# Attention's ramp in a fused attention and tree-FFN kernel: idle products, a split query moved to VectorE, values in another bank, later sums

## What is computed

```python
msg  = h_neigh + E[adj]                       # per target and neighbour
q    = layernorm(x) @ Wq.T + bq               # 8 heads of 16
k, v = msg @ Wk.T + bk, msg @ Wv.T + bv
s    = where(adj == 0, -1e9, q.k / 4)
x    = x + (softmax(s) masked @ v) @ Wo.T + bo
# tree of depth 7: each token takes one path of 8 nodes
h = layernorm(x)
for level in range(8):
    score = h . w1s[node] + b1s[node]
    out  += (h @ w2s[node] + b2s[node]) * gelu(|score|)
    node  = 2 * node + 1 + (score > 0)
x = x + out
```

## Time and profile before

| | us |
|---|---|
| runs of the kernel before | 143.86, 144.15, 145.56; median 144.15 |
| the profiled execution, its whole time | 144.65 |
| its span (first to last record) | 142.70 |
| outside the span | 1.95 |
| busy in the span: PE, DVE, ACT, POOL | 108.8, 98.2, 64.2, 40.4 |
| scores of unit 0 start, end of attention's unit loop on VectorE | 12.23, 62.63 |
| mean granted clock of TensorE | 0.923 of full speed |

### The profile page before, as it was taken

One profiled execution on the slowest core, in us unless ns is written; L12 is line 12 of the kernel. 1 busy time (PEld: TensorE's weight loads), 2 busy tenths in 40 slices (PEclk: granted clock), 3 DMA queues, 4 the chain that ended last, 5 costly groups with the idle time before them and its releaser, 6 DMA issues.

```text
span 142.7 us, 3388 instructions
## 1 busy us (share of the span) xinstructions
PE 108.8 (76%) x958; PEld 74.4 (52%) x959; DVE 98.2 (69%) x292; ACT 64.2 (45%) x132; POOL 40.4 (28%) x84
## 2 busy tenths in 40 slices
PE   6874593499998989978897499688699678787800
PEld 2351431345564646655363165377588577676800
DVE  1779973968778878834888994546536695865670
ACT  3074647438768867922191015245333234243310
POOL 6400002940000000000400017135626245875452
PEclk9999659559999999999999968999999999999985
DMA  3979999999960000008992001100000000000000
GB/s 115 312 253 302 441 441 441 425 413 427 404 262 0 2 5 0 5 0 316 416 432 74 0 0 37 37 5 0 0 2 0 2 0 0 20 17 0 0 18 18
DMA packets 3419, 20.13 MB, mean 141 GB/s; under 512 B 465, under 2 KB 2000, under 8 KB 2896
## 3 DMA queue, kind: packets, MB, share of 16 engines
q1 hardware_dynamic: 2048, 18.42, 31.9%
q10 hardware_dynamic: 1104, 1.05, 2.4%
q0 software_dynamic: 256, 0.52, 1.2%
HBM read 19.47 MB, written 0.52 MB: 140 GB/s over the span
## 4 chain that ended last, share of the span: by engine, by line
PE 29%; DVE 27%; issue 15%; DVEq 13%; ACT 8%; DMA 4%; POOL 3%; POOLq 0%; ACTq 0%
PE turn_ps L653 10%; DVE early L1077 8%; PE s_ps L599 5%; DVEq L83 5%; DVEq L88 5%; ACT prob L465 4%; PE misc_ps L618 2%; POOL early L380 2%; DMA x_sb<-in_x 2%; PE aux_ps L618 2%; DMA early<-x_rows,token_s 2%; PE misc_ps L801 2%; DVE path L998 2%; DVE early L848 2%; PE misc_ps L552 2%
## 5 line engine op out<-in xcount | busy, mean ns | idle before, releaser
L653 PE MATMUL turn_ps<-ident,prob 128*128 128x128 f32 x128 | 22.7, 305 | 8.0 <-ACT prob L465 7.1
L394 POOL TENSOR_TENSOR early<-early,scaled_sb 128x128 f32<-128x128 f32 x48 | 21.1, 455 | 23.4 <-ACT scaled_sb L525 23.2
L465 ACT ACTIVATE prob<-prob,negmax 128x512 f32<-128x512 f32 x32 | 21.7, 715 | 6.7 <-DVE negmax L955 6.7
L653 PEld LDWEIGHTS turn_ps<-ident,prob 128*128 128x128 f32 x128 | 14.9, 151 | 16.9 <-ACT prob L465 14.2
L955 DVE CUSTOM_DVE_ANT_0 prob<-s_ps,mask 128x512 f32<-128x512 f32 x32 | 21.0, 684 | 3.1 <-PE s_ps L599 1.7
L791 PE MATMUL s_ps<-w,msg 128*128 x128 | 18.4, 287 | 5.8 <-issue 4.0
L791 PEld LDWEIGHTS s_ps<-w,msg 128*128 128x128 f32 x128 | 15.5, 191 | 8.5 <-issue 8.4
L1077 DVE SCALAR_TENSOR_TENSOR early<-s_ps,coef,early 128x128 f32<-128x128 f32 x48 | 14.1, 346 | 8.1 <-issue 6.3
L371 POOL TENSOR_TENSOR rstd<-veps,mhalf 128x2 f32<-128x2 f32 x2 | 1.4, 717 | 38.9 <-DVE veps L825 38.9
L1077 DVE SCALAR_TENSOR_TENSOR early<-turn_ps,coef,early 128x128 f32<-128x128 f32 x16 | 5.6, 350 | 9.2 <-issue 9.1
L525 ACT ACTIVATE scaled_sb<-s_ps,coef 128x128 f32<-128x128 f32 x16 | 5.9, 367 | 13.3 <-PE s_ps L791 11.4
(11 more groups left out here) (183 smaller groups left out, 191.8 us busy)
## 6 DMA issues: line engine op xcount, KB each, us to landing
w<-in_w_t SPq DMA_DIRECT2D x3, 4096.0 KB, 22.7
w<-in_w_t SPq DMA_DIRECT2D x1, 4032.0 KB, 12.5
w<-in_adj SPq DMA_DIRECT2D x1, 1024.0 KB, 8.9
w_sb<-in_w_t ACTq DMA_DIRECT2D x1, 384.0 KB, 4.2
x_sb<-in_x SPq DMA_DIRECT2D x1, 256.0 KB, 3.0
msg<-in_neigh_t SPq DMA_DIRECT2D x1, 256.0 KB, 4.0
x_rows<-x ACTq DMA_DIRECT2D x1, 256.0 KB, 9.9
row_sb<-in_rows ACTq DMA_DIRECT2D x1, 255.5 KB, 7.8
```

Source lines behind the costliest of these rows:

```text
L394: nc.gpsimd.tensor_tensor(mine, mine, scaled_sb[:, i, :], ALU.add).then_inc(pooled[i], STEP)
L465: nc.scalar.activation(prob[:, u % RING, :], prob[:, u % RING, :], ACT.Exp, bias=negmax[:, t, h:h + 1], scale=-1.0).then_inc(exped, 1)
L653: last = nc.tensor.transpose(turn_ps[u % 2][:, m * P:(m + 1) * P], prob[:, u % RING, m * P:(m + 1) * P], ident[:])
```

## The change

Six things change; the arithmetic stays the same.

- `FILLERS = (10, 5, 5)` and `keep_clock`: TensorE multiplies the identity by itself, 128 columns of float32, into a bank that is free: ten times after the turning of tiles 1 to 3, five times ahead of the transposes of unit 0 and five times ahead of those of unit 1. In front of the loop TensorE waits for `q_moved[0]`, which stood in the loop at u 1.
- The subtraction of query slice 1 moves from GpSimd to VectorE, into u 6 of its loop (`query_second`). GpSimd's constants come right after the layernorm's powers, and `x_biased` behind them, now early.
- The values go to `aux_ps` rather than `score_ps[2]`. The scores of units 2 and 3 no longer wait for `v_ready`.
- The addition of the value bias (`values`) moves on VectorE from ahead of unit 0's mask to u 4.
- The scores of units 4 to 7 are split in two blocks: units 4 and 5 behind the transposes and queries of u 2, units 6 and 7 at u 4; before, all four stood ahead of the transposes of unit 2.
- `normalise_values` of tiles 0, 1 and 2 is done at u 19, 27 and 32 rather than 15, 23 and 31.

```diff
+NORMALISED = (19, 27, 32)
+FILLERS = (10, 5, 5)
@@ gpsimd
-            pool.wait_ge(q_first[1], 1)
-            nc.gpsimd.tensor_tensor(q_st[:, 1, :, P:], q_f[:, :, P:], q_st[:, 0, :, P:], ALU.subtract
-                                    ).then_inc(q_second[1], 1)
-
-            pool.wait_ge(row_in, 16)
-            pool.wait_ge(h_ready, 2)
-            nc.gpsimd.tensor_tensor(x_sb[:], x_sb[:], row_sb[:, BO:BO + D].unsqueeze(1).to_broadcast([P, TILES, D]),
-                                    ALU.add).then_inc(x_biased, 1)
-
             nc.gpsimd.memset(ones_h[:], 1.0).then_inc(consts2, 1)
...
+            pool.wait_ge(row_in, 16)
+            pool.wait_ge(h_ready, 2)
+            nc.gpsimd.tensor_tensor(x_sb[:], x_sb[:], row_sb[:, BO:BO + D].unsqueeze(1).to_broadcast([P, TILES, D]),
+                                    ALU.add).then_inc(x_biased, 1)
@@ tensor
+            def keep_clock(bank, n):
+
+                for _ in range(n):
+                    nc.tensor.matmul(bank[:, 0:P], ident[:], ident[:], start=True, stop=True)
...
-                last = nc.tensor.matmul(score_ps[2][:, m * D:(m + 1) * D], msg[:, m * P:(m + 1) * P],
+                last = nc.tensor.matmul(aux_ps[:, m * D:(m + 1) * D], msg[:, m * P:(m + 1) * P],
...
             transposes(misc_ps, h_sb, h_turned, *TILE_SLICES[1])
+            keep_clock(score_ps[3], FILLERS[0])
...
-                    if u == 2:
-                        pe.wait_ge(v_ready, 1)
...
+            pe.wait_ge(q_moved[0], SIDE)
             for u in range(UNITS):
                 quad, place = divmod(u, QUAD)
+                if u < 2:
+                    keep_clock(turn_ps[1], FILLERS[1 + u])
...
-                if place == 2 and u + 2 < UNITS:
+                if place == 2 and QUAD < u + 2 < UNITS:
                     scores(u + 2, u + 2 + QUAD)
+                if u == QUAD:
+                    scores(u + 2, u + QUAD)
...
-                if u == 1:
-                    pe.wait_ge(q_moved[0], SIDE)
...
+                if u == 2:
+                    scores(QUAD, QUAD + 2)
@@ vector
+            def query_second(i):
+
+                lo, hi = Q_SLICES[i]
+                dve.wait_ge(q_first[i], 1)
+                nc.vector.tensor_tensor(q_st[:, 1, :, lo:hi], q_f[:, :, lo:hi], q_st[:, 0, :, lo:hi], ALU.subtract
+                                        ).then_inc(q_second[i], 1)
...
                 if u == 4:
                     masks(1)
+                    values()
                 if u == 5:
                     query_mixed(1)
+                if u == 6:
+                    query_second(1)
                 if u == 7:
                     query_third(1)
...
-                if u >= 15 and (u - 15) % HEADS == 0:
-                    normalise_values((u - 15) // HEADS)
+                if u in NORMALISED:
+                    normalise_values(NORMALISED.index(u))
```

More of the change, by code:

```diff
@@ L907, in _ @@
             keys_first(0)
-            dve.wait_ge(q_first[0], 1)
-            nc.vector.tensor_tensor(q_st[:, 1, :, 0:P], q_f[:, :, 0:P], q_st[:, 0, :, 0:P], ALU.subtract
-                                    ).then_inc(q_second[0], 1)
+            query_second(0)
             query_mixed(0)
@@ L915, in _, with values @@
             masks(0)
-            dve.wait_ge(v_done, 1)
-            dve.wait_ge(row_in, 16)
-            dve.wait_ge(v_room, 2)
-            nc.vector.tensor_tensor(v_st[:, :, :, 0:DH], score_ps[2].rearrange("p (m h c) -> p m h c", h=HEADS, c=DH),
-                                    row_sb[:, BV:BV + D].rearrange("p (h c) -> p h c", c=DH).unsqueeze(1
-                                    ).to_broadcast([P, NT, HEADS, DH]), ALU.add).then_inc(v_ready, 1)
+            def values():
+                dve.wait_ge(v_done, 1)
+                dve.wait_ge(row_in, 16)
+                dve.wait_ge(v_room, 2)
+                nc.vector.tensor_tensor(v_st[:, :, :, 0:DH], aux_ps[:].rearrange("p (m h c) -> p m h c", h=HEADS, c=DH),
+                                        row_sb[:, BV:BV + D].rearrange("p (h c) -> p h c", c=DH).unsqueeze(1
+                                        ).to_broadcast([P, NT, HEADS, DH]), ALU.add).then_inc(v_ready, 1)
             def normalise_values(t):
```

## The result

| | before | after |
|---|---|---|
| median of 18 executions each, same chip | 144.39 us | 143.45 us (141.79 to 146.11) |
| the profiled execution | 144.65 | 143.74 |
| span | 142.70 | 141.8 |
| mean granted clock | 0.923 | 0.950 |

The ratio of after to before is 0.9889 with a 95% interval of 0.9855 to 0.9923: 1.1% faster, which is clear of no change but less than the 2% that the prediction asked of a difference. (Ratios leave the disturbed executions out, medians do not.) The forecast was 141.9, a gain of 2.25 us or 1.6%. Within 2% was the likeliest outcome of the forecast (0.61), and it came, with a smaller gain. On the 144.15 of the earlier runs the ratio makes 142.6, inside the forecast's own range of 141.0 to 143.0; the median as measured, 143.45, lies above that range and inside the whole one, 139.6 to 144.1.

The account below looks back on a forecast made before the run. Attention's first eight units, the ramp, with VectorE waits and TensorE clock falls, were taken as where time could be won. Gain 2.5 - 0.7 + 0.4 = 2.2 us: 142.45 profiled, 141.9 median; range 139.6 to 144.1, forecast's own 141.0 to 143.0.

Parts of the forecast that it names:

- The collision, 1.1: Ahead of the first scores: GpSimd's early bias addition stops VectorE's queue once, for 1.1 us (bounds 0 and 1.98).
- rival 1: Ahead of the first scores: no collision, GpSimd waits rather than VectorE; gain 3.0, 141.1 us; chance 0.20.
- The normalising, at nothing: Normalising of tiles 1 to 3, beside GpSimd's early constants: no cost in the forecast's sum.
- rival 5: At the normalising: GpSimd's fills stop VectorE, up to 0.7 more on the path; gain 1.5, 142.6 us; chance 0.08.
- Values at u 4, 0.61: Value addition moved to u 4: costs 0.61 us of VectorE there, where no shadow hides it.
- The ramp's queue, 5.83 and 7.37: VectorE sets the ramp: 5.83 us from unit 0's mask to the later masks, then 7.37 through unit 7's mask.
- Half clock over the first steady quad, 0.7: Units 8 to 11: TensorE's second clock fall stays, costing 0.7 us more (bounds 0 and 1.6).
- Sums, 0.4: Row sums taken four units later: 0.2 us a tile, 0.4 for two tiles (bounds -0.2 and 1.0).
- Behind attention nothing changes; it moves as a whole.: Everything after attention: no change in length, so attention's gain arrives whole at the end.
- 3 (the clock falls at 15 all the same): Before the first scores: a new gap drops TensorE's clock, queries' wait returns; gain about 0.9, 143.2 us; chance 0.15.
- 2 (clock held all through): Attention: TensorE's clock never falls; gain 3.9, 140.2 us, or 139.1 without the collision too; chance 0.14.
- Rival 4: Attention: the clock falls and stays half through the first steady quad; 1.0 lost, 145.1 us; chance 0.05.

Follow-up runs that it names:

- experiment 3: The kernel after without its twenty idle products on TensorE: 145.69 us, ratio 1.0078 against the kernel before.
- experiment 4: The kernel after with the division by row sums back at units 15, 23 and 31: 144.27 us, ratio 0.9928 against the kernel before.
- experiment 7: The kernel after with the scores of units 4 to 7 together again, ahead of unit 2's transposes: 145.00 us, ratio 1.0059 against the kernel before.
- experiment 5: The kernel after with the later queries' subtraction given back to GpSimd, behind its early bias addition: 143.89 us, ratio 0.9968 against the kernel before.
- experiment 6: The kernel after with the value bias added ahead of unit 0's mask again, in the new bank: 143.51 us, ratio 0.9939 against the kernel before.
- experiment 8: The kernel after with eleven more idle products, ahead of unit 4's and 5's transposes and unit 8's scores: 142.73 us, ratio 0.9846 against the kernel before.
- experiment 1: The kernel after with only GpSimd's output bias addition held until the later queries' third part: 143.28 us, ratio 0.9883 against the kernel before.
- experiment 9: The kernel after with GpSimd's constants and bias addition held until the later queries' third part, plus eleven late idle products: 141.46 us, ratio 0.9751 against the kernel before.
- experiment 2: The kernel after with GpSimd's ten constants and bias addition held until the later queries' third part: 142.34 us, ratio 0.9843 against the kernel before.
- experiment 10: Experiment 9 with more idle products in the sorting of tokens, three ahead of the counts and three ahead of the ranks: 142.05 us, ratio 0.9803 against the kernel before.
- experiment 12: Experiment 9 with the scaled query bias made by ScalarE, one VectorE instruction less: 141.32 us, ratio 0.9761 against the kernel before.
- experiment 11: The kernel before with only the change's 20 idle products added: 143.72 us, ratio 0.9928 against the kernel before.

## Why the prediction was right, and where it was wrong

Right was the structure: unit 0 later by a meeting on VectorE, a ramp worth 3.6 (3.93) once its first fall of the clock is filled, the second fall left over and now lying in the steady part, and a small gain of the sums. By its own signs: `x_biased` at 10.34, a VectorE instruction of 1.50 beside it, `query_mixed` 1.02, unit 8's mask at 29.10, tiles of 9.72 and 9.56, full clock from 13 to 28.75. Two signs failed, unit 0's mask (14.59 for 14.2 to 14.4) and the normalising beside a `memset`. And one thing was luck: that 29.10 is the forecast's own figure for unit 8 (see the ramp's queue below).

Step by step:

- *The collision, 1.1.* Its size was right, 1.08, but who waits is decided by hundredths of a microsecond. Seven kernels have the early addition, and in all seven the instruction that starts first runs on. In the kernel after and in experiments 3, 4 and 7 the addition starts 0.05 to 0.07 ahead and takes 1.27 or 1.28, and VectorE loses 1.0 to 1.1. In experiments 5, 6 and 8 VectorE starts 0.06 to 0.23 ahead and loses nothing; the addition takes 1.65 to 1.81, and what is left of it costs VectorE's subtraction 0.35 to 0.58. Timeline of experiment 8:

```profile
9.50 0.74 DVE L859 SCALAR_TENSOR_TENSOR w<-w,from_even 128x512 f32<-128x512 bf16 x1
...
9.56 1.81 POOL L365 TENSOR_TENSOR x_sb<-x_sb,row_sb 128x512 f32<-128x512 f32 x1
...
10.65 1.00 DVE L899 TENSOR_TENSOR early<-w,early 128x256 bf16<-128x256 f32 x1 [0.41 <-ACT early L438]
```

  So rival 1 (GpSimd waits) did not come in the kernel after, but did in three neighbours of it; even there it cost 0.35 to 0.58, not 0. The addition alone takes 1.27 (experiments 1 and 9), so that it stood too in the earlier trace rows, as the prediction read, is right. The prediction also told from the Trainium skill (SBUF — State Buffer, Who interferes with whom) that whoever started first keeps the port. The seven early meetings agree; the earlier trace rows do not, as there VectorE starts 0.04 ahead of the subtraction (23.89 and 23.93) and is the one that stands. What decides at so small a distance is open.
- *The normalising, at nothing.* 0.33 was missing, and that was rival 5, which had a chance of 0.08: the fills do hold up the normalising, 1.38 here and 1.78 in experiment 1 against 0.86 in experiment 2, where no fill runs beside. I had priced it as another case. It was the same case, and it adds. The Trainium skill (SBUF — State Buffer, Who interferes with whom), as the prediction told it, says that `tensor_scalar` in a two-port mode contends with GpSimd, whatever this does. The runs agree: 0.86 alone, 1.38 and 1.78 beside fills.
- *Values at u 4, 0.61.* Nothing, by experiment 6. The rule I broke: a queue that is busy without a gap is not yet the only bound. ScalarE's first part ends at 22.52 in the kernel after and VectorE takes it up at 22.56, so both arrive together, and in experiment 6 what was taken from VectorE came back as a wait of 0.45.
- *The ramp's queue, 5.83 and 7.37.* Measured 5.83 (14.59 to the later masks at 20.42) and 7.30 (to 27.72). But it began 0.3 later than forecast (14.59 for 14.29). The scores of unit 8 then started at 28.13, not within 0.1 of its end but 0.4 later, and took 0.89, not 1.47, as the clock fell at 28.75 only. Two errors on the late side and one on the early side cancel to the 29.1: that is luck.
- *Half clock over the first steady quad, 0.7.* It cost 1.27 against the forecast's own quad of 4.68 (5.95), and 1.40 against the 4.55 of experiment 8, inside the bounds of 0 and 1.6 but near the upper. What was wrong is "some is covered by VectorE's pace": VectorE stood 1.75 for turned units, and most of TensorE's loss (2.2 - 0.64 = 1.56 by the forecast) reached the path.
- *Sums, 0.4.* 0.37 by experiment 4. For the two full tiles of the two kernels 9.72 and 9.56 stand against 9.84 and 9.82, which is 0.38.
- *"Behind attention nothing changes; it moves as a whole."* This is the step that failed. 1.08 was given back: 0.16 from attention's end to the sorted tokens, 0.08 to the first weighted addition, 0.85 in the node loop. Most of the last, 0.7 (44.29 against 43.57), is there at full clock (experiment 10), and it is not due to VectorE's one more instruction alone (experiment 12).

The sum: forecast 142.45 for the profiled execution, measured 143.74. Of the 1.29 between, 0.24 was lost in attention, where errors of 0.3 (unit 0) and 0.4 (half clock) on the one side met 0.3 of a better ramp and 0.1 of later units on the other, and 1.08 behind it (the rest is rounding and the time outside the span).

Of the rivals, 1 (no collision) and 3 (the clock falls at 15 all the same) did not come in the kernel after; 2 (clock held all through) did not come in the profile of the kernel after, though that of experiment 6 shows it: 4.57 from unit 8 to unit 12, and attention's end at 58.83. Rival 4's mechanism, half clock where the steady part begins, is the 1.1 to 1.4 above; the point from which it would decide was not reached in any run. Experiment 3, with no idle products to run at half, is nearest: a fall at 13, full clock again at 23, a second fall at 30, unit 8's mask at 31.73, and slower than before. Rival 5 came, on top of the forecast's case.

## What to carry to other kernels

Fill a thin stretch of TensorE wherever work that depends on it follows, and count on the next thin stretch to bring the fall there: eleven idle products in front of the third quad took 1.3 us out of attention. In the whole time the evidence is weaker: 0.4% alone, with overlapping intervals, and 0.9% where GpSimd's work was out of the way (0.9843 to 0.9751, intervals that just touch; the two further kernels with both, experiments 10 and 12, lie at 0.9803 and 0.9761). Work that an idle engine does "for free" is put where no two-input or normalising instruction of VectorE lies on the path: GpSimd's constants and its addition, wanted 50 us later, cost 1.4 at the start and nothing behind the last split. Where two engines meet within a tenth of a microsecond, price both orders: a small edit elsewhere turned the order round in three of seven kernels here. And when a gain of the front does not arrive at the end, measure the later stages by their own landmarks before blaming the part that was changed.

## What the runs showed that was not expected

**The node loop has two lengths.** In the kernel before, experiment 5 and experiment 11 it takes 43.57, 43.59 and 43.63 us; in all others 44.2 or more: 44.21 to 44.24 in experiments 1, 2, 3 and 7, 44.3 in 10 and 12, 44.42 in the kernel after, and 44.83 to 45.39 in the four where a fall of the clock lies inside. The code of the loop is the same in all. The difference lies in the turns behind the first boundary of a tile. Timeline of the kernel before:

```profile
105.71 0.45 POOL L394 TENSOR_TENSOR early<-early,scaled_sb 128x128 f32<-128x128 f32 x1 [2.60 <-ACT scaled_sb L525]
...
106.97 0.35 DVE L1077 SCALAR_TENSOR_TENSOR early<-misc_ps,coef,early 128x128 f32<-128x128 f32 x1
...
107.63 0.88 DVE L1077 SCALAR_TENSOR_TENSOR early<-s_ps,coef,early 128x128 f32<-128x128 f32 x3 [0.31 <-issue]
...
109.44 0.35 DVE L1077 SCALAR_TENSOR_TENSOR early<-misc_ps,coef,early 128x128 f32<-128x128 f32 x1
```

The same turns in the kernel after:

```profile
104.47 1.43 POOL L392 TENSOR_TENSOR early<-early,scaled_sb 128x128 f32<-128x128 f32 x3 [2.90 <-ACT scaled_sb L523]
...
105.40 0.35 DVE L1094 SCALAR_TENSOR_TENSOR early<-misc_ps,coef,early 128x128 f32<-128x128 f32 x1
...
105.82 0.37 ACT L523 ACTIVATE scaled_sb<-s_ps,coef 128x128 f32<-128x128 f32 x1 [0.67 <-PE s_ps L798]
...
106.65 0.88 DVE L1094 SCALAR_TENSOR_TENSOR early<-s_ps,coef,early 128x128 f32<-128x128 f32 x3 [0.90 <-issue]
...
108.46 0.35 DVE L1094 SCALAR_TENSOR_TENSOR early<-misc_ps,coef,early 128x128 f32<-128x128 f32 x1
```

And in experiment 12, where VectorE's count is back at 292:

```profile
101.59 1.42 POOL L394 TENSOR_TENSOR early<-early,scaled_sb 128x128 f32<-128x128 f32 x3 [3.01 <-ACT scaled_sb L526]
...
103.78 0.88 DVE L1099 SCALAR_TENSOR_TENSOR early<-s_ps,coef,early 128x128 f32<-128x128 f32 x3 [0.90 <-issue]
```

From one addition out of `misc_ps` to the next it is 2.47 us before and 3.06 after, and VectorE's wait ahead of its group of three is 0.90 for "issue", that is for nothing that the profile shows, where it was 0.31. GpSimd is late in the same turn: it starts 0.50 behind the end of the ScalarE result that it adds (103.97), where before it started 0.13 behind (105.58), and does three additions in one go of 1.43 where it did one of 0.45 and then two. ScalarE is not late: its 105.82 comes 2.43 after the turn's first weighted addition (103.39), as in experiment 11, where 106.51 comes 2.43 after 104.08. So two engines start late at one place, while their inputs are there.

What the three kernels with the short loop share is that the subtraction of the later queries is in GpSimd's program (84 instructions, against 83) and not in VectorE's; all eleven kernels without it have the long loop, and steps of 3.06 and 2.75 there. TensorE's count does not decide: experiment 3 has the 958 of the kernel before and the long loop, experiment 11 has 998 and the short one. Experiment 12 excludes that VectorE's count of instructions alone decides. It kept one wait more than the kernel before, and the profile does not count waits, so VectorE's program is not excluded altogether. A kernel with one instruction added to GpSimd was not run; what decides stays open.

One more thing in the traces goes with the length of the loop, in all fourteen kernels: the DMA queue 14, of the kind "instruction", loads 8 KB five times in the span. In the three kernels with the short loop its last two loads are 9.3 to 9.4 us apart (103.86 and 113.18 in the kernel before), with none in the turn above; in the eleven others they are 1.3 to 1.7 apart and both lie in it. The DMA view of the kernel after for 103.4 to 107:

```profile
DMA packets 2, 0.02 MB, mean 5 GB/s; under 512 B 0, under 2 KB 0, under 8 KB 0
...
q14 instruction: 2, 0.02, 1.4%
```

They start at 105.10 and 106.63, the second with VectorE's late group (106.65). Whether they are the reason of the delays or come with the same shift is not shown.

The Trainium skill (Runtime: NRT & Kernel Launch, Instruction fetch mechanics) says that instructions are fetched ahead in order and that a taken branch to a target outside what is held has to fetch first. A loop with branches, late on two engines at one place after their programs were shifted, with two loads of instructions close together just there, would fit; no run here proves it.

**One profile does not tell what the clock does.** Experiment 6 held full clock through attention in its profile with TensorE busy for 1.86 us between 25 and 28.75, where the kernel after, with 1.85 in the same stretch, lost it; yet experiment 6 is no faster than the kernel after (ratios 0.9939 and 0.9889, medians 143.51 and 143.45). The profile of experiment 10 has full clock up to 134 and took 140.75; its median is 142.05. Nor does the mean do: four executions of the kernel after at a mean granted clock of 0.972 to 0.974 took 141.79, 142.14, 142.97 and 143.17, so it matters where the fall lies. A term for the clock is therefore best forecast with both outcomes in its bounds, and judged by medians.
